# New orders of a step in a pipelined adapter, layer norm and conditional linear layer

## The chip, the cores and the metric

The kernel runs on one core of a Trainium2 chip. The metric is the time of one execution on the device in microseconds (us). Each core has TensorE (matmuls, PE), VectorE (DVE), ScalarE (ACT), GpSimd (POOL) and SyncE (SP), each with an instruction queue of its own that runs in order, and 16 DMA engines. The queues wait for one another through semaphores.

## What is computed

```python
# x is (32, 512, 512); two lists of 32 ids choose the weights of each sample
def reference(x, lang, cat, W1, b1, W2, b2, gamma, beta, W, b):
    h = relu(einsum('bsh,bha->bsa', x, W1[lang]) + b1[lang][:, None, :])      # a = 128
    y = x + einsum('bsa,bah->bsh', h, W2[lang]) + b2[lang][:, None, :]
    n = (y - mean(y)) * rsqrt(var(y) + 1e-5)
    x = x + n * gamma[lang][:, None, :] + beta[lang][:, None, :]
    return x + einsum('bti,bio->bto', x, W[cat]) + b[cat][:, None, :]          # W is 512 x 512
```

All is float32.

## The kernel before

A sample is 512 tokens by 512 features: four tiles of 128 tokens (NT = 4, index t) and four chunks of 128 features (NC = 4, index c). The kernel is a software pipeline over the 32 samples, written out by hand. Step k works on three samples at once: the adapter of sample k (up, relu, down, y, statistics), the norm and x1 of sample k - 1, and the linear layer of sample k - 2; besides it prepares sample k + 1. A step function stands in each engine's queue, and is called six times in a loop body (ROUND = 6), since buffers repeat after two or three samples: k.b is k mod 2, k.x is k mod 3. `k.count(per, back, more)` is the count that a semaphore has when "more" of the "per" events of sample k - back are done, so every wait names a sample. Steps 0 and 1 are written out separately ahead of the loops.

To get float32 out of fast matmuls, an operand is split in a high part (ScalarE, rounded to fp32r) and a low part (the rest, by GpSimd or VectorE), and a product is three matmuls: high x high, high x low, low x high (`split_product`, L837). This is done for x and w1 (three of four chunks, the fourth in plain float32, L882), h and w2, x1 and W.

**TensorE** (L927, not changed): linear tiles 0 and 1 of sample k - 2, up of sample k, the transposes of the norm of sample k - 1 for chunks 0 and 1 (`turn_norm`, L857), linear tile 2, down of sample k, transposes for chunks 2 and 3, linear tile 3. Tile 0 waits chunk by chunk for the low parts of x1 (L909), made by VectorE (L732) in the step before. PSUM has eight banks of which the linear layer uses o_bank 0 and 1 in turn, the norm n_bank 0 and 1 in turn.

**ScalarE** (L555): first part of W high (L511, two chunks at a time; it waits for GpSimd's `diag_done`), the norm of four tiles (L501), second part of W high, relu and h high (L528, L531), the issue of two of the four quarter loads of x for sample k + 2 (L591), x1 high for chunks 0 and 1 (L518), w2, w1 and x high for sample k + 1 (L486, L548, L553), squares of y for three tiles (L537), x1 high for chunks 2 and 3, the fourth square, the standard deviation (L542). In step 2 (`k.last(2)`) the norm comes first.

**VectorE** (L747): chunks 0 and 1 of the next x turned into the transposed layout xT (L667, from x_quad, which the quarter loads fill), output tile 0 (L744: bank plus b into out_half), chunks 2 and 3, output tile 1, x1 of chunk 0 (L726), h low (L672), x1 of chunk 1, x1 low for chunks 0 and 1 (L732), output tile 2, y and its means (L681, L687), x1 and x1 low for chunks 2 and 3, output tile 3, and last the statistics: `variance` and `inverse_deviation`, seven small instructions (L700 to L717) of which the second waits for all four squares and the third for the deviation.

**GpSimd** (L397): identity onto the diagonal of W (L405, which gives the residual), b2 onto x in two pairs of tiles (L423) with the low parts of W (L428) between and after, then w2, w1 and x low for sample k + 1 (L382, L388, L394).

**SyncE** (L281) issues the other loads and all stores: two quarters of x for sample k + 2, w1 and w2 of sample k + 1 (after the squares of sample k - 1), W of sample k, b2 and x of sample k + 1, b, the store of the first half of sample k - 2, then, after x1 of sample k - 1, the parameters gamma, beta and b1 of sample k + 1, and the store of the second half.

## Time and profile before

| | us |
|---|---|
| median of 3 runs (lowest, highest) | 615.1 (613.81, 616.61) |
| the profiled execution | 614.85 |
| its span, first to last instruction | 613.0 |

| engine | busy us | share of the span |
|---|---|---|
| TensorE matmuls | 606.5 | 99% |
| VectorE | 520.0 | 85% |
| GpSimd | 520.9 | 85% |
| ScalarE | 512.9 | 84% |
| DMA, mean of 16 engines | | 8 to 9 tenths in nearly all slices |

The clock granted to TensorE is 9 tenths or more in every slice (1.00 over nearly all of the span). 166.22 MB are moved, 271 GB/s on average. The page gives shares of the whole span; the stretches and single steps are read from the trace, where a line's rows tell its start, its length and, in brackets, the idle time of its engine before it and what ended that. A matmul's recorded end lies beyond the next one's start, as they are pipelined: only starts are compared.

### The profile page before, as it was taken

The page shows a single profiled execution, that of the slowest core. Times are in us where ns is not written, and L with a number is a line of the kernel's source. Part 1 is how long each engine was busy: PE and PEld are TensorE (multiplying, and loading weights), DVE is VectorE, ACT ScalarE, POOL GpSimd, SP SyncE. Part 2 cuts the span into 40 slices and gives each one's busy share as a digit, 9 for nine tenths or more (in the row PEclk, how much of TensorE's full clock was granted, in tenths as well). Part 3 has the DMA queues.
Part 4 walks back from the last instruction along what each step waited for, and adds up shares of the span by engine and source line. Part 5 has one row for each costly group of instructions (what it writes and reads, how often), then busy time and mean ns, then how long its engine had stood idle before and what let it go on. Part 6 is the DMA issues. An engine that isn't in the chain of part 4 may idle for free.

```text
span 613.0 us, 10710 instructions
## 1 busy us (share of the span) xinstructions
PE 606.5 (99%) x2863; PEld 488.4 (80%) x2863; DVE 520.0 (85%) x1151; ACT 512.9 (84%) x770; POOL 520.9 (85%) x263
## 2 busy tenths in 40 slices
PE   9999999999999999999999999999999999999998
PEld 7676787778888877787888888888888888888887
DVE  1799979889899889898888899899898889898673
ACT  4878888889888889889989889889888889889770
POOL 6778889899888899889999898899888899889830
PEclk9999999999999999999999999999999999999999
DMA  8989799887998898899898998888898898998422
GB/s 302 251 258 307 258 311 300 277 265 253 296 307 274 270 300 253 298 287 289 269 294 268 305 303 265 283 290 270 301 303 278 283 295 253 301 308 273 156 87 103
DMA packets 125938, 166.22 MB, mean 271 GB/s; under 512 B 11062, under 2 KB 72768, under 8 KB 121812
## 3 DMA queue, kind: packets, MB, share of 16 engines
q1 hardware_dynamic: 94900, 150.12, 75.2%
q10 hardware_dynamic: 30912, 15.73, 9.1%
q8 instruction: 10, 0.16, 0.1%
q14 instruction: 20, 0.16, 0.1%
q0 software_dynamic: 96, 0.05, 0.0%
HBM read 132.17 MB, written 33.55 MB: 270 GB/s over the span
## 4 chain that ended last, share of the span: by engine, by line
PE 75%; DMA 7%; ACT 6%; SPq 5%; DVE 3%; issue 3%; POOL 1%; ACTq 0%; DVEq 0%; POOLq 0%
PE o_bank L839 15%; PE o_bank L841 15%; PE o_bank L840 15%; PE n_bank L857 7%; DMA x_tok<-in_x 6%; PE d_bank L839 4%; PE d_bank L841 4%; PE d_bank L840 4%; PE d_bank L882 3%; ACT norm L501 2%; PE y_bank L839 2%; PE y_bank L841 2%; PE y_bank L840 2%; DVE x1T_lo L732 2%; DMA x_quad<-in_x 1%
## 5 line engine op out<-in xcount | busy, mean ns | idle before, releaser
L839 PE MATMUL o_bank<-w_hi,x1T_hi 128*128 128x512 f32 x512 | 205.6, 402 | 0.5 <-DVE x1T_lo L732 0.5
L841 PE MATMUL o_bank<-w_hi,x1T_lo 128*128 128x512 f32 x512 | 200.1, 391 | 0.0
L840 PE MATMUL o_bank<-w_lo,x1T_hi 128*128 128x512 f32 x512 | 199.1, 389 | 0.0
L428 POOL TENSOR_TENSOR w_lo<-w_raw,w_hi 128x1024 fp32r<-128x1024 f32 x62 | 149.1, 2404 | 10.0 <-ACT w_hi L511 9.8
L667 DVE STREAM_TRANSPOSE xT<-x_quad 128x512 f32<-128x512 f32 x120 | 127.2, 1101 | 34.1 <-DMA x_quad<-in_x 34.1
L501 ACT ACTIVATE norm<-y,neg_mean_rstd,rstd 128x512 f32<-128x512 f32 x128 | 152.2, 1266 | 1.1 <-DVE neg_mean_rstd L717 1.1
L423 POOL TENSOR_TENSOR x_tok<-x_tok,b_bc 128x1024 f32<-128x1024 f32 x60 | 145.0, 2416 | 5.4 <-DMA x_tok<-in_x 2.9
L518 ACT ACTIVATE x1T_hi<-n_bank,params 128x512 fp32r<-128x512 f32 x126 | 84.5, 688 | 34.7 <-DVE n_bank L726 29.5
L839 PEld LDWEIGHTS o_bank<-w_hi,x1T_hi 128*128 128x128 f32 x512 | 96.3, 188 | 21.1 <-issue 3.1
L841 PEld LDWEIGHTS o_bank<-w_hi,x1T_lo 128*128 128x128 f32 x512 | 96.1, 188 | 21.0
L840 PEld LDWEIGHTS o_bank<-w_lo,x1T_hi 128*128 128x128 f32 x512 | 96.4, 188 | 17.6
L537 ACT ACTIVATE x_tok<-y,neg_mean 128x512 f32<-128x512 f32 x128 | 91.8, 718 | 17.9 <-DVE neg_mean L687 17.8
L726 DVE SCALAR_TENSOR_TENSOR n_bank<-n_bank,params,xT 128x512 f32<-128x512 f32 x126 | 91.9, 754 | 10.1 <-PE n_bank L857 10.0
L394 POOL TENSOR_TENSOR xs_lo<-xT,xs_hi 128x1536 fp32r<-128x1536 f32 x28 | 98.7, 3525 | 0.0
L732 DVE SCALAR_TENSOR_TENSOR x1T_lo<-n_bank,params,x1T_hi 128x512 fp32r<-128x512 f32 x126 | 90.5, 748 | 9.3 <-ACT x1T_hi L518 4.5
L744 DVE TENSOR_TENSOR out_half<-o_bank,b_bc 128x512 f32<-128x512 f32 x127 | 85.4, 673 | 11.9 <-PE o_bank L841 11.7
L511 ACT ACTIVATE w_hi<-w_raw 128x1024 fp32r<-128x1024 f32 x64 | 67.7, 1061 | 18.2 <-POOL w_raw L405 17.4
L382 POOL TENSOR_TENSOR w_lo<-w_raw,w_hi 128x512 fp32r<-128x512 f32 x31 | 40.3, 1300 | 48.6 <-ACT w_hi L486 48.6
L857 PEld LDWEIGHTS n_bank<-ident,norm 128*128 128x128 f32 x504 | 58.9, 145 | 11.4 <-ACT norm L501 4.7
L857 PE MATMUL n_bank<-ident,norm 128*128 128x128 f32 x504 | 66.2, 274 | 0.6 <-ACT norm L501 0.5
L405 POOL TENSOR_TENSOR w_raw<-w_raw,ident 128x512 f32<-128x512 f32 x32 | 50.3, 1571 | 0.0
L681 DVE SCALAR_TENSOR_TENSOR y<-d_bank,x_tok 128x512 f32<-128x512 f32 x64 | 43.8, 684 | 1.1 <-PE d_bank L841 1.1
(95 smaller groups left out, 812.3 us busy)
## 6 DMA issues: line engine op xcount, KB each, us to landing
w_raw<-in_L_cond_W SPq DMA_DIRECT2D x32, 1024.0 KB, 6.6
out<-out_half SPq DMA_DIRECT2D x63, 512.0 KB, 4.5
x_tok<-in_x SPq DMA_DIRECT2D x31, 1024.0 KB, 11.4
w_raw<-in_L_cond_W SPq DMA_DIRECT2D x64, 256.0 KB, 4.3
b_bc<-in_L_cond_b SPq DMA_DIRECT2D x64, 256.0 KB, 8.7
x_quad<-in_x SPq DMA_DIRECT2D x62, 256.0 KB, 3.8
x_quad<-in_x ACTq DMA_DIRECT2D x58, 256.0 KB, 10.7
x_tok<-in_x ACTq DMA_DIRECT2D x2, 256.0 KB, 3.3
```

The source lines that it names most:

```text
L394: pool.tensor_tensor(xs_lo[:, :, :], xT[(k.x + 1) % 3][:, 0:NS, :], xs_hi[:, :, :].bitcast(F32), ALU.subtract).then_inc(xs_lo_done, 1)
L423: pool.tensor_tensor(pair, pair, b2_bc[p][:, :].rearrange("p (o h) -> p o h", o=1).to_broadcast([P, 2, H]), ALU.add).then_inc(x_b2_done, 2)
L428: pool.tensor_tensor(w_lo[q][:, c:c + 2, :], w_raw[q][:, c:c + 2, :], w_hi[q][:, c:c + 2, :].bitcast(F32), ALU.subtract).then_inc(w_lo_don ...
L501: act.activation(dst, src, ACT.Identity, scale=rstd[:, t:t + 1], bias=neg_mean_rstd[:, t:t + 1]).then_inc(norm_done, 1)
L537: act.activation(x_tok[k.b][:, t, :], y[:, t, :], ACT.Square, bias=neg_mean[:, t:t + 1], accum_out=sq_sum[:, t:t + 1]).then_inc(sq_done, 1)
L667: dve.transpose(xT[(k.x + 1) % 3][:, c, :].rearrange("p (b j) -> p b j", j=SQ), x_quad[1 - k.b][:, :, c::NC]).then_inc(xT_done, 1)
L726: dve.scalar_tensor_tensor(norm_bank(k, c)[:, :], norm_bank(k, c)[:, :], params[q][:, c:c + 1], xT[(k.x + 2) % 3][:, c, :], ALU.mult, ALU. ...
L732: dve.scalar_tensor_tensor(x1T_lo[q][:, c, :], norm_bank(k, c)[:, :], params[q][:, NC + c:NC + c + 1], x1T_hi[q][:, c, :].bitcast(F32), AL ...
L839: pe.matmul(acc, lhs_hi, rhs_hi, start=first, stop=False)
L840: pe.matmul(acc, lhs_hi, rhs_lo, start=False, stop=False)
L841: return pe.matmul(acc, lhs_lo, rhs_hi, start=False, stop=last)
L857: ins = pe.transpose(norm_bank(k, c)[:, t * P:(t + 1) * P], norm[:, t, c * P:(c + 1) * P] if by_chunk(k) else norm[:, t, c::NC], ident[:, :])
```

## The change

Five orders are changed; no matmul, no arithmetic and no byte of traffic is added or removed, but for a third small buffer of parameters.

- ScalarE: the norm whole, then w2's high part of the next sample, then both parts of W; the quarter loads leave its queue; all four squares and the deviation come ahead of x1's high parts of chunks 2 and 3.
- VectorE: output tile 0 and 1 each come ahead of a pair of turned chunks rather than behind it; h low behind x1 of chunk 1; the statistics ahead of x1's low parts of chunks 2 and 3.
- GpSimd: both sums of b2 and x first, then w2's low part, then both low parts of W, then w1's and x's as before.
- SyncE: w1 and w2 wait for down of sample k - 1; the wait for the squares stands ahead of b2 and x only; then the store of the second half of sample k - 3, b, the parameters (one of three buffers, waiting for x1 of sample k - 2), all four quarter loads of x, and the store of the first half of sample k - 2.
- Steps 0 and 1 keep their orders, but ScalarE issues no quarter loads there.

The core of the diff; the lines with @@ name the place.

```diff
@@ params: three buffers, and so three semaphores params_in
-        params = [sb(f"params{i}", [P, NP]) for i in range(2)]
+        params = [sb(f"params{i}", [P, NP]) for i in range(3)]
...
@@ SyncE, step
-                if quads:
-                    sp.wait_ge(xT_done, k.count(NC, 0, NC))
-                    load_x_quads(k.sample(-2), p)
                 if loads:
-                    sp.wait_ge(sq_done, k.count(NT, 0, 0))
+                    sp.wait_ge(down_done, k.count(NT, 0, 0))
                     load_w1(lang, q)
                     load_w2(lang, q)
                 if w_load:
...
                     load_w(cat_w, p)
                 if loads:
+                    sp.wait_ge(sq_done, k.count(NT, 0, 0))
                     load_b2(lang, q)
                     load_x(k.sample(-1), q)
+                if linear and k.since(3):
+                    store(k, 3, 1)
                 if turn:
...
                     load_b(cat_b, q)
+                if loads:
+                    if k.since(2):
+                        sp.wait_ge(x1_lo_done, k.count(NC, 1, 0))
+                    load_params(lang, (k.x + 1) % 3)
+                if quads:
+                    sp.wait_ge(xT_done, k.count(NC, 0, NC))
+                    load_x_quads(k.sample(-2), p)
                 if linear:
                     store(k, 2, 0)
-                if loads:
-                    sp.wait_ge(x1_lo_done, k.count(NC, 0, 0))
-                    load_params(lang, q)
-                if linear:
-                    store(k, 2, 1)
...
@@ GpSimd, step
                     if adapter:
                         plus_b2_pair(0)
+                        plus_b2_pair(2)
+                    if follow:
+                        low_w2(q, k.count(1, -1, 1))
                     if turn:
                         low_w_pair(0)
-                    if adapter:
-                        plus_b2_pair(2)
-                    if turn:
                         low_w_pair(2)
-                if follow:
-                    low_w2(q, k.count(1, -1, 1))
-                    if k.since(3):
+                    if follow and k.since(3):
                         low_w1(k)
                         low_xs(k)
...
@@ ScalarE, step
-                if k.last(2):
-                    for t in range(NT):
-                        normalise(k, t)
-                    high_w(k, 0)
-                else:
-                    high_w(k, 0)
-                    for t in range(NT):
-                        normalise(k, t)
+                for t in range(NT):
+                    normalise(k, t)
+                if follow:
+                    high_w2_of_next(k)
+                high_w(k, 0)
                 high_w(k, 2)
                 if adapter:
                     relu(k)
-                if follow and not k.last(S - 2):
-                    load_next_x_quads(k)
                 high_x1(k, 0)
                 high_x1(k, 1)
-                if follow:
-                    high_w2_of_next(k)
-                    if k.since(3):
-                        high_w1_of_next(k)
-                        high_xs_of_next(k)
+                if follow and k.since(3):
+                    high_w1_of_next(k)
+                    high_xs_of_next(k)
                 if adapter:
-                    square(k, 0)
-                    square(k, 1)
-                    square(k, 2)
+                    for t in range(NT):
+                        square(k, t)
+                    deviation(k)
                 high_x1(k, 2)
                 high_x1(k, 3)
-                if adapter:
-                    square(k, 3)
-                    deviation(k)
...
@@ VectorE, step
                 else:
+                    output(k, 0)
                     if follow:
                         turn_next_x(k, 0)
                         turn_next_x(k, 1)
-                    output(k, 0)
+                    output(k, 1)
                     if follow:
                         turn_next_x(k, 2)
                         turn_next_x(k, 3)
-                    output(k, 1)
                     x1(k, 0)
-                    if adapter:
-                        low_h(k)
                 x1(k, 1)
+                if adapter and not k.last(2):
+                    low_h(k)
                 low_x1(k, 0)
                 low_x1(k, 1)
                 output(k, 2)
...
                 x1(k, 2)
                 x1(k, 3)
+                if adapter:
+                    variance(k)
+                    inverse_deviation(k)
                 low_x1(k, 2)
                 low_x1(k, 3)
                 output(k, 3)
-                if adapter:
-                    variance(k)
-                    inverse_deviation(k)
```

## Rows read from the trace of the kernel before

**Rows 1.** Busy time in stretches: stretch, us, engines (instructions), clock, DMA share, GB/s

```profile
54.60:297.30 242.70, 242.12 (x1130) 192.96 (x1129) 214.78 (x470) 210.79 (x313) 218.70 (x105) 1.00 0.87 282
297.30:573.30 276.00, 276.00 (x1307) 224.86 (x1306) 245.50 (x540) 245.50 (x362) 252.00 (x121) 1.00 0.88 282
```

**Rows 2.** Timeline, TensorE: start us, us, what; feeding y, and R

```profile
433.12 0.39 PE L841 MATMUL d_bank<-w_hi,hT_lo 128*128 128x512 f32 x1
...
439.05 0.39 PE L839 MATMUL o_bank<-w_hi,x1T_hi 128*128 128x512 f32 x1
```

**Rows 3.** Waits (us, times, longest), 54 to 297 us, then 297 to 573 us

```profile
PEld n_bank L857 <- ACT norm L501: 4.0, 10, 0.9
...
DVE xT L667 <- DMA x_quad<-in_x: 16.6, 13, 1.9
```

**Rows 4.** Timeline, TensorE and VectorE: tile 0's first, x1T_lo, tile 1's first; two steps

```profile
198.24 0.39 PE L839 MATMUL o_bank<-w_hi,x1T_hi 128*128 128x512 f32 x1
...
198.46 1.41 DVE L732 SCALAR_TENSOR_TENSOR x1T_lo<-n_bank,params,x1T_hi 128x512 fp32r<-128x512 f32 x2
...
200.96 0.39 PE L839 MATMUL o_bank<-w_hi,x1T_hi 128*128 128x512 f32 x1
...
235.35 0.39 PE L839 MATMUL o_bank<-w_hi,x1T_hi 128*128 128x512 f32 x1
...
235.87 1.41 DVE L732 SCALAR_TENSOR_TENSOR x1T_lo<-n_bank,params,x1T_hi 128x512 fp32r<-128x512 f32 x2
...
238.24 0.39 PE L839 MATMUL o_bank<-w_hi,x1T_hi 128*128 128x512 f32 x1
```

**Rows 5.** Timeline, VectorE, the step of R = 420.65: x1, low_h, y, low_x1

```profile
429.75 0.76 DVE L726 SCALAR_TENSOR_TENSOR n_bank<-n_bank,params,xT 128x512 f32<-128x512 f32 x1 [0.47 <-PE n_bank L857]
...
430.55 0.69 DVE L672 TENSOR_TENSOR hT_lo<-d_bank,hT_hi 128x512 fp32r<-128x512 f32 x1
...
433.98 0.68 DVE L681 SCALAR_TENSOR_TENSOR y<-d_bank,x_tok 128x512 f32<-128x512 f32 x1
...
438.40 1.41 DVE L732 SCALAR_TENSOR_TENSOR x1T_lo<-n_bank,params,x1T_hi 128x512 fp32r<-128x512 f32 x2
```

**Rows 6.** Timeline, ScalarE's squares in that step; sample 0's last square and statistics

```profile
435.44 0.72 ACT L537 ACTIVATE x_tok<-y,neg_mean 128x512 f32<-128x512 f32 x1 [0.49 <-DVE neg_mean L687]
...
436.16 0.71 ACT L537 ACTIVATE x_tok<-y,neg_mean 128x512 f32<-128x512 f32 x1
...
18.46 0.72 ACT L537 ACTIVATE x_tok<-y,neg_mean 128x512 f32<-128x512 f32 x1
...
20.45 0.16 DVE L717 TENSOR_TENSOR neg_mean_rstd<-d_bank,rstd 128x4 f32<-128x4 f32 x1
```

**Rows 7.** Timeline of step 2: ScalarE's W parts, VectorE, and TensorE's wait

```profile
37.85 2.00 ACT L511 ACTIVATE w_hi<-w_raw 128x1024 fp32r<-128x1024 f32 x2
...
41.05 0.69 DVE L672 TENSOR_TENSOR hT_lo<-d_bank,hT_hi 128x512 fp32r<-128x512 f32 x1 [0.73 <-ACT hT_hi L531]
...
45.14 0.68 DVE L681 SCALAR_TENSOR_TENSOR y<-d_bank,x_tok 128x512 f32<-128x512 f32 x1
...
49.48 1.41 DVE L732 SCALAR_TENSOR_TENSOR x1T_lo<-n_bank,params,x1T_hi 128x512 fp32r<-128x512 f32 x2
...
50.38 0.47 PE L839 MATMUL o_bank<-w_hi,x1T_hi 128*128 128x512 f32 x1 [0.49 <-DVE x1T_lo L732]
```

**Rows 8.** Start: VectorE's first turn of sample 2; DMA traffic from 19 to 36 us

```profile
22.46 1.10 DVE L667 STREAM_TRANSPOSE xT<-x_quad 128x512 f32<-128x512 f32 x1 [1.85 <-DMA x_quad<-in_x]
...
DMA packets 4171, 4.50 MB, mean 265 GB/s; under 512 B 471, under 2 KB 3015, under 8 KB 4039
```

**Rows 9.** The page's groups and DMA issues, whole span

```profile
L501 ACT ACTIVATE norm<-y,neg_mean_rstd,rstd 128x512 f32<-128x512 f32 x128 | 152.2, 1266 | 1.1 <-DVE neg_mean_rstd L717 1.1
...
L428 POOL TENSOR_TENSOR w_lo<-w_raw,w_hi 128x1024 fp32r<-128x1024 f32 x62 | 149.1, 2404 | 10.0 <-ACT w_hi L511 9.8
...
x_quad<-in_x ACTq DMA_DIRECT2D x58, 256.0 KB, 10.7
```

More of the change, by code:

```diff
@@ L338, in _ @@
                          ).then_inc(first_b1_in[1], 16)
-            load_x_quads(2, 0, range(NQ))
+            load_x_quads(2, 0)
             sp.wait_ge(table_done, 1)
@@ L357, in _ @@
             last = Step(S // ROUND, 3)
+            store(last, 3, 1)
             store(last, 2, 0)
```

33 lines of the change are left out of this document (14 added, 19 removed).

## The prediction

> **What bounds the kernel now.** I read, in this order, the busy time in four stretches, the waits of the same stretches, one step on each engine in the timeline, then the first 55 us.
>
> From 297.3 to 573.3 us TensorE is busy for 276.0 of 276.0 us over 15 steps (1307 matmuls, 87 in a step): 18.40 us a step, no gap. From 54.6 to 297.3 us 13 steps take 242.7 us, 18.67 each [rows 1]. So the later half stands at TensorE's own work, and the change, which takes no matmul away, can win only what the earlier half has over it: 242.7 - 13 x 18.40 = 3.5 us. I count offsets in a step from R, the first matmul of tile 0 of the linear layer: R is 439.05 in one step and 420.65 in the one before [rows 2]. The earlier half loses its 3.5 us in two places: the weight loads of the norm's transposes waited 4.0 us for ScalarE's norm, ten times, and tile 0's third chunk waited for VectorE's x1T_lo [rows 3, 4]. In the later half VectorE waits 16.6 us for x_quad [rows 3], about 1.1 us a step, but TensorE has no gap there, so this wait costs nothing.
>
> The second place has a limit that can be read. With the third x1T_lo started at R + 0.22 (198.46) tile 0 takes its usual 2.72 us. Started at R + 0.52 (235.87) it takes 2.89, 0.17 more [rows 4]. So TensorE loses s - 0.35 us when that instruction starts s behind R. In the step at 439.05 it starts at 438.40, s = -0.65: a full microsecond of room [rows 2, 5].
>
> **The parts of the change.**
>
> Norm ahead of W's first part (ScalarE), statistics ahead of x1's last parts (VectorE), W's parts last on GpSimd. The norm no longer waits for the high part of W, which waits for GpSimd's diagonal, and its scale comes some 2 us earlier. The waits on the norm go. Worth at most the 3.5 us; part of that is the other place, and one of the 13 steps lost nothing, so I take 3.0.
>
> GpSimd keeps every instruction. The new wait is that of w2's low part for w2's high part, now ahead of both parts of W; behind it stand W's low parts and w1's and x's. Norm ends near offset 5.5, w2's high part at 6.0, then GpSimd needs 1.2 us for w2 (half as wide as a part of W) and 2 x 2.4 for W [rows 9], and is at w1 near 12.0, which is when it comes. Cost nothing: W's low part is needed only in the next step (18.4). If that cover goes it costs what GpSimd is late, from 6 us on.
>
> ScalarE: the two quarter loads leave it (whose issue held x1's high part back), and the fourth square and the deviation move ahead of x1's third and fourth high part. Nothing there becomes late: x1's high parts then end near 19.0, the norm's four instructions (1.27 us on average, [rows 9]) end at 24.0, that is 5.6 of the next step, and the first x1 behind their transposes stands at 9.10.
>
> VectorE: the first output now precedes the first two turns. It waits for tile 0 (near 2.9) and then two turns, an output and two turns end near 8.2, before x1 can start at 9.10 (429.75) [rows 2, 5]. Nothing.
>
> Then the one part that lies on the path: the five small instructions of the statistics, with their waits for all four squares, now stand **ahead of the third x1T_lo**, whose room is 1.0 us. Worked out from x1 at 9.10: two in a row take 1.41 us of 0.75 each, so a successor starts 0.09 before the recorded end [rows 5]. x1 twice 1.32, low_h 0.60, low_x1 twice 1.32, output 0.60: y starts at 12.94. The matmul that feeds it starts at 12.47 and is 0.39 long [rows 2], so it is ready. Before, y started at 13.33 (433.98), as x1's high parts were late. The first square starts 1.46 behind y (435.44 - 433.98), the second 0.72 behind it [rows 5, 6]; the third waits for the second pair's mean, 2.97 behind y; the fourth at 16.63. The statistics' last product starts 1.99 us after the fourth square where nothing else stands between (18.46 to 20.45 in the first sample), and the next instruction starts 0.09 before its end, 0.08 behind its start, as it is 0.16 long [rows 6]. The third x1T_lo then starts at 16.63 + 2.07 = 18.70, that is s = 0.30, against the limit of 0.35. **The room of 1.0 us is used up but for 0.05.** Both numbers are good to about 0.1. From below the cost is 0; from above, with s = 0.55, 0.2 us in each of 28 steps, 5.6 us. It can't gain, as TensorE has no gap to give. I take 0.02 a step, 0.5 us, since a few steps will lie beyond. It is a loop: y waits for TensorE, which waits for x1T_lo, so a loss is paid in every step.
>
> The first steps. In step 2 the room doesn't exist: TensorE already waits 0.49 us there for x1T_lo, started at 49.48, 4.34 us behind y (45.14) [rows 7]. In the new order it is 3.69 + 2.07 = 5.76 behind y: **1.4 us later**, and nothing hides it. Besides, low_h in this step waited for ScalarE (0.73 us, at 41.05) [rows 7], and in ScalarE's queue w2's high part for sample 3 now stands ahead of both parts of W and of the relu. In before it came after. Its own slot is 0.5 us (an estimate: a square of the same size starts 0.72 behind the last with its accumulator's read in between, [rows 6]); it also waits for w2 to land. SyncE now issues w1, w2, W, b2, x, b, then sample 3's four quarters, then step 2's w1 and w2: 4.5 MB behind sample 2's quarters, which were in at 22.46. At 265 GB/s that is 17 us: 39.4, where ScalarE is there at 37.85 [rows 7, 8]. A wait of 1 to 1.5 us, of which I take 1.2. Bounds: 0 if w2 overtakes the quarters, 2.5 if the queue is no faster than 230 GB/s. So step 2 costs 1.4 + 0.5 + 1.2 = **3.1 us**, bounds 1.9 and 4.4, and TensorE never makes it good.
>
> All quarters on SyncE, behind x, b and the parameters. ScalarE's took 10.7 us to land [rows 9], being issued last of 4 MB. Now they are issued near offset 4 of a step and wanted at 3.5 of the next, 18 us later, so VectorE's wait for them goes, worth nothing. SyncE's queue: the four issues stand ahead of the store of half 0 and of the next step's w1 and w2, which aren't wanted until 15 us later. The second half's store waits for the last output at about 2.2 and holds b and the parameters back, both of which have a step of room. The third parameter buffer takes a wait away and costs nothing. The Trainium skill (DMA: Bandwidth & Descriptors, "Issuing engines are not separate DMA queues" and "Queues, rings and completion order") says that transfers of both engines run on the same 16 DMA engines and that within one ring they are taken in order. By that rule no bandwidth is won, and what is issued behind the quarters waits for them; it speaks for the late w2 in step 2, and against the bound of 0 there (by the rule alone the sum would keep its 1.2 us).
>
> End: after the last step TensorE runs without a wait; the new order of stores changes nothing of the last one.
>
> **Sum.** The profiled execution took 614.85 us, its span 613.0, against a median of 615.1. 614.85 - 3.0 + 3.1 + 0.5 = 615.4 us. So the change wins in the earlier half what it pays in step 2.
>
> **The rivals.**
>
> Statistics decide (slower): s is not 0.30 but 0.45 to 0.65, from waits on semaphores that my spacings leave out. It decides from s = 0.35 on. At s = 0.50 it is 28 x 0.15 = 4.2 us, 619.1 us. For it: the room is 0.05 us. Against it: every spacing is a measured one.
>
> The start is cheap: w2 lands in time or the order in step 2 costs half. 614.85 - 3.0 + 1.0 to 1.9 = 612.9 to 613.8 us. For it: the landing is estimated from a mean rate, and transfers differ much in theirs.
>
> Full gain: the stall in step 2 is absent, as work shifts beside it, and the 3.5 us come back: 611.4 us. Against it: y to x1T_lo in that step is a plain chain.
>
> One queue for all loads: the quarters block SyncE's queue, stores land late, and the output that reuses the half waits. A half is stored again 9 to 10 us after its issue at offset 2.3; ahead of it lie 2.75 MB of loads, about 10 us at 265 GB/s. It decides once the queue is 2 us later than I take it; 0.2 us a step would give 28 x 0.2 = 5.6 us, 621.0 us.
>
> That the orders do nothing (the earlier half keeps its loss from transfers, step 2 pays): 618.4 us.
>
> **How the numbers follow.** A measurement of this kernel tells about 0.5%, 3.1 us, from no change. Forecast 0.47, statistics 0.20, cheap start 0.15, full gain 0.08, queue 0.04, orders do nothing 0.06. All of the forecast and most of the cheap start lie within 3.1 us of 615.1; the full gain and a few in a hundred of the cheap start are faster; statistics, queue and half of the last are slower. That gives 0.12 faster, 0.62 same, 0.26 slower. The range 612.2 to 619.8 reaches over the cheap start and over most of the statistics case, and leaves out the full gain and the queue.
>
> **What would show it.** Steps from 75 us on of 18.40 us, with no wait on the norm. The third x1T_lo at s near 0.3; beyond 0.35 each step is longer by the excess. In step 2 TensorE's wait for x1T_lo near 2 us, low_h near 42.8 rather than 41.05, w2's high part waiting for a DMA, and the first up behind it near 57.6 rather than 54.6. VectorE's wait for x_quad gone. The prediction is wrong if a new wait of GpSimd on w2 reaches TensorE, if s misses by more than 0.1, or if w2 lands before 37.9.

## The result and the profile after the change

The changed kernel takes **618.14 us** (median of 5 runs, 615.9 to 618.49), the kernel before 613.81 us beside it: ratio 1.006, 95% interval 1.0031 to 1.0089. It is slower, by a little over the 0.5% that can be told, and 2.7 us above the forecast of 615.4. Against the kernel before the miss is larger: the forecast added 0.6 us to the profiled execution's 614.85, and 4.3 us were added to the 613.81 measured beside it. The profiled execution took 618.28 us, its span 616.5.

| first "up" matmul of a step, us | step 2 | step 3 | step 4 | last | 27 steps from step 4 on | span |
|---|---|---|---|---|---|---|
| before | 28.96 | 54.58 | 73.49 | 573.30 | 499.81 | 613.0 |
| after | 31.33 | 58.78 | 77.68 | 576.76 | 499.08 | 616.5 |
| difference | +2.4 | +4.2 | +4.2 | +3.5 | -0.7 | +3.4 |

So the whole loss, and more, is there 78 us into the run: 2.4 us in the start, 1.8 in step 2. The other 27 steps give 0.7 back, where 2.5 was forecast. Busy time in stretches (stretch, us, engines with their instructions, granted clock, DMA share, GB/s), of the kernel after, which answer to [rows 1] but for the first:

```profile
20.00:30.00 10.00, 8.03 (x39) 6.43 (x38) 6.29 (x17) 7.49 (x12) 6.08 (x6) 0.83 0.96 265
54.60:297.30 242.70, 242.69 (x1140) 196.15 (x1141) 219.15 (x474) 211.48 (x315) 218.89 (x105) 1.00 1.03 286
297.30:573.30 276.00, 274.37 (x1297) 222.42 (x1296) 247.13 (x539) 238.78 (x360) 249.32 (x120) 1.00 1.00 279
```

The first of these in the kernel before:

```profile
20.00:30.00 10.00, 8.56 (x53) 7.17 (x52) 7.86 (x22) 8.49 (x14) 6.04 (x6) 1.00 0.96 253
```

The earlier half, the one the change aimed at, now holds 1140 matmuls in place of 1130 and has no gap. The later half, full before, holds ten fewer (1297 for 1307) and has a gap of 1.6 us. In the start the granted clock is 0.83, where it was 1.00. The start and step 2 on TensorE (start us, us, what, and in brackets the idle time ahead of it and what ended it):

```profile
24.99 0.50 PE L824 MATMUL d_bank<-w_hi,hT_hi 128*128 128x512 f32 x1 [1.98 <-DVE hT_lo L657]
...
28.35 0.63 PE L825 MATMUL d_bank<-w_lo,hT_hi 128*128 128x512 f32 x1
28.77 0.63 PE L826 MATMUL d_bank<-w_hi,hT_lo 128*128 128x512 f32 x1
...
44.68 0.50 PE L824 MATMUL d_bank<-w_hi,hT_hi 128*128 128x512 f32 x1 [0.56 <-DVE hT_lo L657]
...
54.58 0.47 PE L824 MATMUL o_bank<-w_hi,x1T_hi 128*128 128x512 f32 x1 [1.79 <-DVE x1T_lo L717]
```

TensorE was idle for 1.98 us ahead of the down projection of step 1 (1.44 before), ran at full speed for 1.7 us, and then at the lower of its two levels: matmuls 0.42 us apart (28.35 to 28.77) instead of 0.23, from 26.6 to 29.2 us (1.2 in place of 2.4 GHz). Then VectorE and ScalarE in the same stretch, which answer to [rows 7] and [rows 8]:

```profile
23.27 1.10 DVE L652 STREAM_TRANSPOSE xT<-x_quad 128x512 f32<-128x512 f32 x1 [2.37 <-DMA x_quad<-in_x]
...
40.20 0.63 ACT L493 ACTIVATE w_hi<-w_raw 128x512 fp32r<-128x512 f32 x1
...
43.94 0.69 DVE L657 TENSOR_TENSOR hT_lo<-d_bank,hT_hi 128x512 fp32r<-128x512 f32 x1 [1.52 <-ACT hT_hi L538]
...
48.03 0.68 DVE L666 SCALAR_TENSOR_TENSOR y<-d_bank,x_tok 128x512 f32<-128x512 f32 x1
...
53.70 1.40 DVE L717 SCALAR_TENSOR_TENSOR x1T_lo<-n_bank,params,x1T_hi 128x512 fp32r<-128x512 f32 x2
```

The third x1T_lo of step 2 starts 5.67 us behind y (forecast 5.76, before 4.34). Its wait is the 1.79 us of TensorE. The high part of w2 (40.20) hardly waits: w2 landed at 40.18, and ScalarE was free at 40.07, 2.2 us later than before.

A step of the later half, tile 0's first matmul (R) at 442.56, which answers to [rows 2, 5, 6]:

```profile
433.25 1.42 DVE L711 SCALAR_TENSOR_TENSOR n_bank<-n_bank,params,xT 128x512 f32<-128x512 f32 x2 [0.70 <-PE n_bank L842]
...
437.08 0.69 DVE L666 SCALAR_TENSOR_TENSOR y<-d_bank,x_tok 128x512 f32<-128x512 f32 x1
...
440.86 0.71 ACT L544 ACTIVATE x_tok<-y,neg_mean 128x512 f32<-128x512 f32 x1
...
442.56 0.39 PE L824 MATMUL o_bank<-w_hi,x1T_hi 128*128 128x512 f32 x1
...
442.91 1.40 DVE L717 SCALAR_TENSOR_TENSOR x1T_lo<-n_bank,params,x1T_hi 128x512 fp32r<-128x512 f32 x2
```

The chain came out as forecast: y 3.83 us behind x1 (forecast 3.84), the fourth square 3.78 behind y (forecast 3.69), the third x1T_lo 2.05 behind that (forecast 2.07). It starts at s = 442.91 - 442.56 = 0.35, 0.27 in the steps outside the loop (forecast 0.30). Such steps last 18.41 and 18.37 us. The waits from 77 to 577 us (us in total, times, longest), which answer to [rows 3]:

```profile
POOL w_lo L389 <- ACT w_hi L493: 44.3, 27, 3.1
...
DVE out_half L729 <- DMA out<-out_half: 2.1, 2, 1.4
PE o_bank L824 <- DVE x1T_lo L717: 1.6, 2, 1.2
```

VectorE's wait for x_quad and TensorE's for the norm are gone. GpSimd's wait for w2's high part, which the prediction calls new, was there before at nearly the same size: 48.6 us over the whole span, against 52.9 now. From the page of the kernel before:

```profile
L382 POOL TENSOR_TENSOR w_lo<-w_raw,w_hi 128x512 fp32r<-128x512 f32 x31 | 40.3, 1300 | 48.6 <-ACT w_hi L486 48.6
```

New is that VectorE's output waited twice for a store. TensorE's gap in the later half follows from that, and SyncE's queue shows why (issues of DMAs; start, length, what):

```profile
351.68 0.41 SPq L282 DMA_DIRECT2D out<-out_half  x1
...
353.55 8.63 SPq L247 DMA_DIRECT2D x_quad<-in_x  x4
...
428.93 4.36 SPq L247 DMA_DIRECT2D x_quad<-in_x  x4
433.38 2.24 SPq L282 DMA_DIRECT2D out<-out_half  x1
```

```profile
363.00 0.69 DVE L729 TENSOR_TENSOR out_half<-o_bank,b_bc 128x512 f32<-128x512 f32 x1 [1.44 <-DMA out<-out_half]
```

The store of the second half, issued at 351.68 behind w1, w2, W, b2 and x in the same queue, landed at 362.90, after 11.2 us (the median of the stores on the page is 8.1, and was 4.5 before), and the output that writes this half again, the third of the step, waited 1.44 us for it. How full the queue is can be seen in the issues themselves: the four quarters take SyncE 4.36 us in the step shown, 5.4 in the median step, and 8.63 in this one. In the kernel before SyncE's two quarters cost 0.90 us (and ScalarE's two 0.95):

```profile
425.41 0.90 SPq L243 DMA_DIRECT2D x_quad<-in_x  x2
```

The page's rows that answer to [rows 9] (line, engine, operation, count | busy us, mean ns | idle before; and the DMA's issues with KB and us to landing):

```profile
L508 ACT ACTIVATE norm<-y,neg_mean_rstd,rstd 128x512 f32<-128x512 f32 x128 | 152.3, 1265 | 1.1 <-DVE neg_mean_rstd L702 1.1
...
L435 POOL TENSOR_TENSOR w_lo<-w_raw,w_hi 128x1024 fp32r<-128x1024 f32 x62 | 147.5, 2402 | 12.1 <-ACT w_hi L518 12.1
...
x_quad<-in_x SPq DMA_DIRECT2D x120, 256.0 KB, 9.1
```

No large group of instructions has become longer by more than 2% on average.

### The profile page after: what moved, and what is told of

It is laid out like the page before. It is cut to its first block, busy times and chain, and to the rows that moved or that the text cites. A ratio compares the mean times of both kernels' runs of the same rounds, so it can differ in the third digit from the quotient of the medians.

```text
span 616.5 us, 10723 instructions
## 1 busy us (share of the span) xinstructions
PE 606.5 (98%) x2863; PEld 490.2 (80%) x2863; DVE 525.1 (85%) x1151; ACT 506.4 (82%) x770; POOL 520.8 (84%) x263
## 4 chain that ended last, share of the span: by engine, by line
PE 86%; DMA 5%; DVE 4%; ACT 2%; issue 2%; SPq 1%; DVEq 0%; ACTq 0%
PE o_bank L824 17%; PE o_bank L826 17%; PE o_bank L825 17%; PE n_bank L842 8%; PE d_bank L824 5%; PE d_bank L826 5%; PE d_bank L825 5%; PE d_bank L867 4%; DMA out<-out_half 4%; PE y_bank L824 2%; PE y_bank L826 2%; PE y_bank L825 2%; PE d_bank L855 1%; ACT x_tok L544 1%; DMA w_raw<-in_L_cond_W 1%
## 5 line engine op out<-in xcount | busy, mean ns | idle before, releaser
L435 POOL TENSOR_TENSOR w_lo<-w_raw,w_hi 128x1024 fp32r<-128x1024 f32 x62 | 147.5, 2402 | 12.1 <-ACT w_hi L518 12.1
L729 DVE TENSOR_TENSOR out_half<-o_bank,b_bc 128x512 f32<-128x512 f32 x127 | 86.8, 684 | 33.1 <-PE o_bank L826 30.7
L711 DVE SCALAR_TENSOR_TENSOR n_bank<-n_bank,params,xT 128x512 f32<-128x512 f32 x126 | 89.0, 753 | 20.9 <-PE n_bank L842 20.9
L717 DVE SCALAR_TENSOR_TENSOR x1T_lo<-n_bank,params,x1T_hi 128x512 fp32r<-128x512 f32 x126 | 88.3, 743 | 0.6 <-ACT x1T_hi L525 0.5
L525 ACT ACTIVATE x1T_hi<-n_bank,params 128x512 fp32r<-128x512 f32 x126 | 80.0, 682 | 9.0 <-DVE n_bank L711 7.6
L389 POOL TENSOR_TENSOR w_lo<-w_raw,w_hi 128x512 fp32r<-128x512 f32 x31 | 40.5, 1306 | 52.9 <-ACT w_hi L493 52.9
L518 ACT ACTIVATE w_hi<-w_raw 128x1024 fp32r<-128x1024 f32 x64 | 64.1, 1056 | 0.0
```

Source lines behind the costliest of these rows:

```text
L435: pool.tensor_tensor(w_lo[q][:, c:c + 2, :], w_raw[q][:, c:c + 2, :], w_hi[q][:, c:c + 2, :].bitcast(F32), ALU.subtract).then_inc(w_lo_don ...
L711: dve.scalar_tensor_tensor(norm_bank(k, c)[:, :], norm_bank(k, c)[:, :], params[(k.x + 2) % 3][:, c:c + 1], xT[(k.x + 2) % 3][:, c, :], AL ...
L717: dve.scalar_tensor_tensor(x1T_lo[q][:, c, :], norm_bank(k, c)[:, :], params[(k.x + 2) % 3][:, NC + c:NC + c + 1], x1T_hi[q][:, c, :].bitc ...
```

## The experiments

The theory after the result: the loss has two places, the start and step 2, and the gain in the later steps is small because most executions of the kernel before don't have the loss that the profiled one had. The rival: the steps pay, by the statistics ahead of x1T_lo or by the one queue. Each experiment is compared with runs of the kernel before on its own chip: 613.28 us (17 runs) for the first four, 613.03 (23) for the next four, 613.72 (35) for the last four.

**The changed kernel again.** No edit.

> The changed kernel once more, beside the kernels that it is compared with. Account so far, from its first trace, against the kernel before (span 616.5 against 613.0, +3.4): start up to step 2's first up matmul +2.4 (of which 1.5 under a granted clock of half), step 2 +1.8, the 27 steps after it -0.7 (the 3.0 of the earlier half and 0.8 of a slightly shorter step won, 0.5 lost to statistics in time, 2.6 lost in four steps where VectorE waited for a store). If the start is chance, the span varies with the clock: 614 to 615 us at clock 1.00. If it belongs to the change, the clock is under 1.00 in nearly every run and the first up of step 2 stands near 31.3 us again. Ratio 1.004 to 1.008.

Measured: 618.25 us, ratio 1.0079 (1.0055 to 1.0104). In its trace:

```profile
26.47 0.79 PE L824 MATMUL d_bank<-w_hi,hT_hi 128*128 128x512 f32 x1 [3.66 <-DVE hT_lo L657]
...
56.90 0.47 PE L824 MATMUL o_bank<-w_hi,x1T_hi 128*128 128x512 f32 x1 [1.81 <-DVE x1T_lo L717]
```

```profile
79.97:576.98 497.01, 496.99 (x2350) 403.68 (x2349) 445.25 (x971) 433.51 (x649) 452.99 (x216) 1.00 1.02 283
```

The start is worse here (3.66 us idle, clock 0.78 from 20 to 30 us, step 3 at 61.07). Step 2 takes 27.13 us, 1.5 more than in the kernel before, with the same wait for x1T_lo (1.81 us). The 27 steps take 497.01 us without a wait for a store, and the clock was under 1.0 in 5 of these 6 runs, as expected if the start belongs to the change. The store waits come in some executions alone: of the ten traces here that keep the change's order of stores, the first has 2.1 us of them, one more 0.24 us, the others none. Of the four long steps that the expectation puts down to them, two (18.64 and 18.49 us) hold no such wait and are long in this trace too.

**Step 2 in the old order.** VectorE, ScalarE and GpSimd keep the old place of statistics, fourth square and w2's parts in this one step.

```
-                if adapter:
+                if adapter and not k.last(2):
                     variance(k)
                     inverse_deviation(k)
                 low_x1(k, 2)
                 low_x1(k, 3)
                 output(k, 3)
+                if k.last(2):
+                    variance(k)
+                    inverse_deviation(k)
```

> The changed kernel with step 2 alone in the old order (statistics behind x1's low parts, w2's high and low part late, fourth square late), all other steps new. My theory (step 2 is a fill cost of its own, of statistics ahead of x1's low parts and of w2 in ScalarE's queue): step 2 shrinks from 27.45 to about 25.6 us, the whole by 1.8 to 2.5 us against the changed kernel. The rival (step 2 is late only because the start was late, and its length is set by transfers): no change, 0.5 us at most.

Measured: 615.26 us, ratio 1.0028 (1.001 to 1.0046), 3.0 us less than the changed kernel on that chip.

```profile
49.58 0.68 DVE L674 SCALAR_TENSOR_TENSOR y<-d_bank,x_tok 128x512 f32<-128x512 f32 x1
...
53.92 1.41 DVE L725 SCALAR_TENSOR_TENSOR x1T_lo<-n_bank,params,x1T_hi 128x512 fp32r<-128x512 f32 x2
```

```profile
54.81 0.47 PE L835 MATMUL o_bank<-w_hi,x1T_hi 128*128 128x512 f32 x1 [0.52 <-DVE x1T_lo L725]
...
74.64 0.47 PE L835 MATMUL o_bank<-w_hi,x1T_hi 128*128 128x512 f32 x1 [0.31 <-DVE x1T_lo L725]
```

y to x1T_lo is 4.34 us again, as in the kernel before, and step 2 takes 25.37 us for the 27.13 of the repeat. But step 3 takes 19.84 for 18.90: its norm, now whole and first, waits 1.40 us for statistics that come late, and TensorE waits once more for x1T_lo. In the trace the edit saves 1.76 - 0.94 = 0.8 us; the medians give 3.0. What the medians have beyond it goes with the clock: it was 1.0 or 0.999 in 6 of these 12 runs (five at 1.0 with a median of 613.76) and in 1 of the 6 of the changed kernel. Step 2's order can't act on the clock of the stretch ahead of it, so part of the 3.0 is likely chance among few runs.

**Statistics last in all steps.** VectorE's statistics and ScalarE's fourth square and deviation go behind x1's last parts again; the norm stays whole and first.

```
                 x1(k, 2)
                 x1(k, 3)
-                if adapter:
-                    variance(k)
-                    inverse_deviation(k)
                 low_x1(k, 2)
                 low_x1(k, 3)
                 output(k, 3)
+                if adapter:
+                    variance(k)
+                    inverse_deviation(k)
```

> The changed kernel with the statistics back behind x1's low parts and the last output on VectorE, and the fourth square and deviation back behind x1's high parts on ScalarE, in all steps; norm still ahead of W. My theory (the statistics use up a room of 1.0 us, so that every small delay on VectorE reaches TensorE): the third x1T_lo starts about 0.65 us ahead of tile 0 instead of 0.27 behind it, no step is over 18.45 us, the store waits of VectorE remain but cost nothing; step 2 is 1.4 us shorter. Together 3.5 to 4.5 us less than the changed kernel. The rival (norm is late without the early statistics, or the excess steps come from the queue alone): steps of 18.5 to 18.7 remain, and at most 1.5 us is won.

Measured: 621.81 us, ratio 1.0136 (1.0113 to 1.0158), 3.6 us more than the changed kernel where 3.5 to 4.5 less was expected. The theory that this order costs in the steps fell: s does drop to -0.37, but steps take 18.5 to 18.6 us. Waits from 60 to 577 us:

```profile
ACT norm L508 <- DVE neg_mean_rstd L705: 39.5, 28, 1.5
...
DVE hT_lo L660 <- ACT hT_hi L538: 23.2, 27, 1.1
...
PEld d_bank L827 <- DVE hT_lo L660: 8.6, 24, 0.6
```

ScalarE stands at the norm, and all behind it in its order (w2, both parts of W, the relu) is late, until TensorE waits for hT_lo. So the two orders belong together: with the norm whole and first, the early statistics are needed.

**Two quarter loads back on ScalarE**, behind its relu; the loads of a step on SyncE stay where the change put them. In step 1 ScalarE issues its two behind w2's high part.

```
+                if follow and not k.last(S - 2):
+                    load_next_x_quads(k)
                 high_x1(k, 0)
...
             high_w2_of_next(k1)
+            load_next_x_quads(k1)
```

> The changed kernel with two of the four quarter loads back in ScalarE's queue behind the relu, as before; all else new. Two theories give opposite signs. If the limit of the third x1T_lo is real (a step longer by its start less 0.35 us), the issue holds x1's high part back by 0.4 us, x1T_lo starts near 0.65, and each of 28 steps is 0.3 us longer: 6 to 9 us more than the changed kernel, with no wait for a store. If instead the one queue is what costs, this undoes it and wins 2 to 3 us.

Measured: 628.18 us, ratio 1.0248 (1.0225 to 1.0271), 9.9 us more than the changed kernel. Timeline and stretches:

```profile
51.05 0.79 PE L838 MATMUL d_bank<-w_hi,hT_hi 128*128 128x512 f32 x1 [8.35 <-DVE hT_lo L671]
```

```profile
48.35 2.08 DVE L666 STREAM_TRANSPOSE xT<-x_quad 128x512 f32<-128x512 f32 x2 [9.44 <-DMA x_quad<-in_x]
```

```profile
40.00:50.00 10.00, 2.70 (x12) 1.88 (x10) 1.65 (x2) 2.22 (x4) 10.00 (x6) 0.88 1.13 270
297.30:573.30 276.00, 275.90 (x1297) 221.65 (x1296) 246.67 (x538) 240.21 (x360) 250.99 (x120) 1.00 1.00 283
```

ScalarE's two quarters of sample 3, issued in step 1 at 33.63 and 34.00, landed at 43.76 and 48.33, VectorE stood 9.44 us for them, and step 2 took 35.48 us. That is 8.4 us over the repeat's 27.13, and most of what was lost. The number came near the 6 to 9 us expected, but from a cause that the expectation doesn't have: the 27 steps, to which it gave the loss, took 500.88 us, 3.9 over the repeat, and the start was 4.3 shorter (first up of step 2 at 29.68 for 33.94). There was no wait for a store. The DMA engines' share stayed at 0.99 to 1.00 in the later steps and a store's median landing at 8.3 us, though the quarters are on two queues again.

The later steps settle the limit of [rows 4] on more points: in this and the other traces s = 0.27, 0.35, 0.45, 0.65, 0.86 goes with steps of 18.37, 18.41, 18.47, 18.67, 18.85 us. The excess over 18.37 is 0.04, 0.10, 0.30, 0.48, that is s - 0.35, to 0.03. It is a lower bound where other waits come on top, as in many steps of the run with the store first, below.

**The low part of h first in the start.**

```
-            turn_next_x(k1, 0)
             low_h(k1)
+            turn_next_x(k1, 0)
             turn_next_x(k1, 1)
```

> The changed kernel with one line of the start moved: VectorE makes sample 1's low part of h before it turns sample 2's first chunk, so that down no longer waits for sample 2's last quarter load. My theory (in the changed kernel that quarter lands at 23.2 to 24.7 us instead of 22.4, TensorE stands idle 2.0 to 3.7 us instead of 1.4, and the clock granted to it falls to half behind the longer idle time, 1.5 to 3 us more): TensorE waits under 1 us there, the clock is 1.00 in all runs, step 2's first up matmul stands near 28 us instead of 31.3 to 33.9, and the whole is 2.5 to 4 us less than the changed kernel, 614.5 to 615.5 us. The rival (the clock falls for another cause, and the start is caught up later): clock under 1.00 in most runs again, at most 1 us won.

Measured: 617.85 us, ratio 1.007 (1.0042 to 1.0097): 0.4 below the changed kernel's repeat, far less than expected. The start has no idle of note in this trace and its first up of step 2 stands at 28.09, as expected, but:

```profile
45.41 0.50 PE L824 MATMUL d_bank<-w_hi,hT_hi 128*128 128x512 f32 x1 [3.45 <-DVE hT_lo L657]
```

```profile
40.93 0.63 ACT L493 ACTIVATE w_hi<-w_raw 128x512 fp32r<-128x512 f32 x1 [3.03 <-DMA w_raw<-in_L_cond_W]
```

Here is the wait for w2 that the prediction put into step 2, and larger: ScalarE is there at 37.90, w2 lands at 40.9. In the changed kernel it was hidden by the late start. The two don't add up; take one away and the other comes forward. The clock was 1.0 in 1 of the 6 runs and 0.994 to 0.997 in the others, so both signs of the expectation's rival (clock under 1.00 in most runs, at most 1 us won) came true. That the start's idle time is what lowers the clock is therefore not shown by this run alone; the wait of 3.45 us may do it in the other executions, and in the run below that takes both under 1 us the clock is 1.0 in 10 of 12.

**The second half's store first.**

```
+                if linear and k.since(3):
+                    store(k, 3, 1)
                 if loads:
                     sp.wait_ge(sq_done, k.count(NT, 0, 0))
                     load_b2(lang, q)
                     load_x(k.sample(-1), q)
-                if linear and k.since(3):
-                    store(k, 3, 1)
```

> The changed kernel with SyncE's store of the second half of sample k - 3 ahead of the loads of b2 and x instead of behind them. My theory (VectorE's output waits for this store behind 2.75 MB of loads in one queue, 0.6 to 1.4 us in a few steps, and as the room is gone each wait reaches TensorE): no wait of VectorE for a store, no step over 18.5 us but one or two, 0.5 to 2.5 us less than the changed kernel. The rival (it is the amount of traffic, not its order, that makes these steps long): the long steps remain, or x arrives late on GpSimd, no gain.

Measured: 637.29 to 653.6 us in six runs, with a median of 645.18; the ratio, 1.0424 (1.038 to 1.0468), is taken from the three shortest of them (median 640.12). It is the opposite of what I expected. Waits from 60 to 577 us of an execution of 650.5 us:

```profile
DVE out_half L729 <- DMA out<-out_half: 59.8, 25, 5.6
...
ACT w_hi L493 <- DMA w_raw<-in_L_cond_W: 25.0, 19, 3.8
```

The store waits for an output, SyncE with it, and b2, x, b, parameters and quarters go out later in every step. The next step's store and w2 are then late. So stores and loads that hold one another up on SyncE are a mechanism that works; how near the changed kernel is to it is not shown.

**Sample 3's quarters first in step 1**, ahead of w1 on SyncE, in this step alone.

```
+                if k.last(1):
+                    sp.wait_ge(xT_done, k.count(NC, 0, NC))
+                    load_x_quads(k.sample(-2), p)
                 if loads:
                     sp.wait_ge(down_done, k.count(NT, 0, 0))
                     load_w1(lang, q)
...
-                if quads:
+                if quads and not k.last(1):
```

> The changed kernel with sample 3's four quarter loads ahead of w1, w2 and W in SyncE's step 1 alone, as the kernel before had two of them; all other steps new. It tells why sample 2's last quarter lands late. My theory (the loads issued next behind it decide it: quarters behind quarters leave it at 22.4 us, w1, w2 and W take bandwidth from it): it lands near 22.5 us, TensorE's idle time is 1.4 to 1.6 us and the clock 1.00, the start is 1.5 to 2.5 us shorter; but W and x come 3 us later, which step 2 may pay. The rival (it lands late by chance of that run or by the new code): 23 to 24.7 us again and clock under 1.00.

Measured: 615.57 us, ratio 1.0038 (1.0018 to 1.0057), 2.3 us less than the 617.85 of the run beside it, the clock at 1.0 in 7 of 12 runs.

```profile
24.82 0.50 PE L827 MATMUL d_bank<-w_hi,hT_hi 128*128 128x512 f32 x1 [1.57 <-DVE hT_lo L660]
...
30.54 1.98 PE L858 MATMUL d_bank<-xT,w_raw 128*128 128x512 f32 x4 [0.78 <-DMA w_raw<-in_L_cond_W]
```

1.57 us idle, and the clock stays at 1.00 from 20 to 30 us. But the quarter landed at 23.07, not near 22.5, so the theory that the loads behind it decide its landing fell. And w1 now stands behind four quarters, and TensorE waits 0.78 us for it.

**The kernel before with the low part of h first.** The same edit of the start as above, in the kernel before.

> The kernel before with the same line of the start moved (low part of h ahead of the turn), nothing of the change. It has an idle time of 1.4 us there at full clock. If that idle time is plain loss: 1 to 1.5 us less than the kernel before, near 612 us, clock 1.00. If step 2 is bound by ScalarE's and VectorE's own chains anyway: no difference.

Measured: 613.17 us, ratio 0.9991 (0.9973 to 1.0008), no difference. The first up of step 2 comes 0.9 us earlier (28.04 for 28.96), and by step 3 that is gone (54.48 for 54.58). What the run shows is the loop. 27 steps of the kernel before, in the execution of the prediction and in this one:

```profile
73.49:573.30 499.81, 499.23 (x2351) 403.40 (x2350) 442.22 (x972) 440.06 (x650) 453.55 (x217) 1.00 0.88 282
```

```profile
73.70:570.87 497.17, 497.11 (x2351) 404.49 (x2350) 442.41 (x971) 440.64 (x650) 453.81 (x217) 1.00 0.88 284
```

The same code in the loop takes 499.81 us in one execution and 497.17 in another, in which most steps take 18.40. The changed kernel's 497.01 is hardly less.

**Step 2 old, and sample 3's quarters first.** Both edits above.

> The changed kernel with two edits together: sample 3's quarter loads first on SyncE in step 1 alone, and step 2 alone in the kernel before's order of statistics and w2's high part. Theory (the loss has two places, the start with its half clock and step 2, and the earlier half of every later step is worth next to nothing): the loss of the two places goes together, the first up matmul of step 3 starts at 55.5 to 56.5 us (57.72 with the first edit alone), the time is 612.5 to 613.8 and the granted clock 1.0 in most runs. Rival (the edits remove the same wait twice, as their single results of -3.0 and -2.7 each already reach 615.3 to 615.6): 615 to 616. Second rival (the orders inside the steps are worth 3 us once start and step 2 are mended, as the prediction had it): 610 to 611.

Measured: 614.95 us, ratio 1.002 (1.0002 to 1.0037). The time misses what was expected by over a microsecond and stands beside the first rival's 615 to 616. Step 3 starts at 55.05, earlier than expected, but takes 19.73 us for 18.90, as in the run with step 2 alone. Clock 1.0 in 6 runs (median 613.7), 0.997 in 6 (615.8).

**Step 2 old, and the low part of h first.**

> The changed kernel with the start's low part of h ahead of the turning of sample 2, and step 2 alone in the kernel before's order. Theory (w2's high part pinned ahead of W's in ScalarE is what held step 2 in the run with the first edit alone, by the 3.03 us that it waited for w2 to land): TensorE's 3.45 us idle ahead of down of step 2 goes, the first up of step 3 starts at 56 to 57 us, the time is 612.5 to 614 with the granted clock 1.0 in most runs. Rival (the late landing of sample 3's quarters, which both edits leave behind b on SyncE, decides step 2): idle of 2 to 3 us stays at another place, and the time is 615 to 616.5, no better than with step 2 alone.

Measured: 614.92 us, ratio 1.0031 (1.0008 to 1.0054), 0.9 above what was expected, with the clock at 1.0 in 10 of 12 runs. TensorE's idle ahead of down falls from 3.45 to 0.97 us, as the theory has it (ScalarE no longer stands at w2), and step 3 starts at 56.26. Yet step 3 takes 20.09:

```profile
72.16 0.47 PE L835 MATMUL o_bank<-w_hi,x1T_hi 128*128 128x512 f32 x1 [0.64 <-DVE x1T_lo L725]
```

With the clock full, 1.2 us of loss against the kernel before is left, and it lies in steps 2 and 3: the clock is not the whole of it.

**All three edits.** The loop stays as the change has it.

> All three edits together: start's low part of h first, sample 3's quarters first on SyncE in step 1, step 2 alone in the kernel before's order; the later steps stay wholly as the change has them. Theory: first up of step 3 at 54.6 to 55.5 us, time 611.5 to 613, within 0.5% of the kernel before, because the 27 periods from step 4 on take the same 497 to 499 us in both kernels. Rival (earlier half of each step worth 3 us): 609.5 to 610.5, faster by 0.4 to 0.6%.

Measured: 613.27 us, ratio 0.9983 (0.9965 to 1.0), not to be told from the kernel before, and 0.3 above what was expected. Clock 1.0 in 7 of 12 runs. Step 3 starts at 56.37, 0.9 later than expected. The trace still holds a loss ahead of step 4 (75.57 against 73.49):

```profile
30.11 3.61 PE L869 MATMUL d_bank<-xT,w_raw 128*128 128x512 f32 x4 [2.05 <-DMA w_raw<-in_L_cond_W]
```

The quarters ahead of w1 delay w1 by 2.05 us now that TensorE comes for it in time, and behind this wait the granted clock was 0.83 from 30 to 40 us. The 27 steps take 497.18 us. So the changed kernel's loss of 0.6 to 0.8% lies in the start and step 2 (an edit of step 2 moves part of it to step 3), and with most of it mended the new orders of the later steps win about what is left of it.

**SyncE's step 1 alone, in the kernel before.** Its two quarter loads of sample 3 go behind the load of b.

```
-                if quads:
+                if quads and not k.last(1):
                     sp.wait_ge(xT_done, k.count(NC, 0, NC))
                     load_x_quads(k.sample(-2), p)
...
                     load_b(cat_b, q)
+                if k.last(1):
+                    sp.wait_ge(xT_done, k.count(NC, 0, NC))
+                    load_x_quads(k.sample(-2), p)
```

> The kernel before with one thing changed, in step 1 alone: SyncE's two quarter loads of sample 3 go from the head of the step to behind the load of b; all else stays. Theory (the order of SyncE in step 1 sets when sample 2's last quarter lands, by what is put on the queue ahead of or beside it, and with it TensorE's idle time and clock in the start): the last quarter of sample 2 lands at 23.0 to 24.7 us instead of 22.44, TensorE is idle 2 us or more ahead of down of step 1, the granted clock of the 20 to 30 us window is under 0.9, and the time is 1.5 to 3 us above the kernel before: 614.5 to 616. Rival (it is the changed kernel's one queue for all quarters that lands them late, not their order in step 1): no difference that can be measured, 612.5 to 613.7.

Measured: 613.43 us, ratio 1.0007 (0.9982 to 1.0032). My theory of the start fell:

```profile
24.58 0.53 PE L842 MATMUL d_bank<-w_hi,hT_hi 128*128 128x512 f32 x1 [1.21 <-DVE hT_lo L675]
```

Sample 2's last quarter lands at 22.81, TensorE is idle for 1.21 us, the clock stays at 1.00. The order of SyncE in step 1 by itself doesn't spoil the start. What does is **open**. That quarter landed at 22.44, 22.81 and 23.16 in three traces with the kernel before's program, and at 22.87 to 24.72 in the eleven traces of the changed kernel and its variants (median 23.2), though it is issued at 13.6 to 14.4 in all fourteen. The expectation's rival, the one queue for all quarters, can't be it: the kernel before too has all four quarters of sample 2 on SyncE, behind the same loads, and ScalarE's first quarter load goes out only at 32.91.

What the traces do show is that these same loads kept the DMA engines busier, in the kernel before (first row) and after:

```profile
18.00:22.00 4.00, 4.00 (x21) 2.60 (x20) 1.41 (x10) 2.99 (x8) 3.72 (x3) 1.00 0.95 197
...
18.00:22.00 4.00, 4.00 (x20) 2.52 (x19) 1.69 (x10) 3.00 (x7) 4.00 (x4) 1.00 1.18 189
```

Here nearly all that moves is these quarters. The share is 0.95 to 0.99 in the three traces with the kernel before's program and 1.13 to 1.23 in the eleven others. In the traces' packet records, from 100 to 560 us, the quarters' packets (512 bytes) take 31 ns on average in those three and 44 to 52 in these eleven, while packets of 2048 bytes take 98 to 104 in all. What all eleven have from the start on, and the three don't, is the third parameter buffer. It is declared right ahead of x_quad, and may shift x_quad and all that follows in memory. That this is the cause is a rival that no run tests; the kernel before with an unused third buffer would test it.

The 27 steps took 499.75 us here, so two of the three traces of the old loop have that loss; but this execution took 615.16 us, 1.7 above its own median. Seven of the eight traces with the change's later steps left as they are took 497.0 to 497.4 us.

## Why the prediction was right and wrong

**What bounds the kernel**: right. Steps stand at TensorE's own work in both kernels.

**Norm first, W last, worth 3.0 us**: the waits on the norm went, as forecast. The size was right against the execution it was read from (499.81 - 497.01 = 2.8, where the forecast, less its 0.5 for the statistics, was 2.5) and wrong as a gain on the median. That execution took 614.85 us, 1.0 to 1.8 above the medians of 613.0 to 613.8 that the kernel before showed later, and one of three executions of its loop had next to nothing of the loss. An estimate for the median one: 613.7 us on the last occasion, less 1.8 outside the span, 39.7 behind the last up and 73.7 ahead of step 4 leave 498.5 for the 27 steps, so the gain is 1.4 us. This is the first mis-sized term. In the changed kernel's own profile 2.1 us went to store waits besides.

**GpSimd, ScalarE and the first output cost nothing**: right. But GpSimd's wait for w2's high part isn't new, as the prediction has it: it was 48.6 us before and is 52.9 now, and nobody waited for it. That the third parameter buffer "costs nothing" was given without a reason and isn't shown (the rival above).

**Statistics ahead of x1T_lo**: right to 0.1 us, s = 0.27 to 0.35 against 0.30, and so was the limit of 0.35. The cost came out at 1.0 us at most for the 0.5 forecast (497.01 less 27 steps of 18.37): 0.02 to 0.05 in an ordinary step of the loop, and 0.1 to 0.3 in three steps, six apart, which the forecast lacked. Against that, a step without a wait takes 18.37 us where it took 18.40, 0.8 us in 27 steps, which the forecast lacked too. The "statistics decide" rival (619.1 us) is out: the time is near, the mechanism isn't there.

**The first steps, 3.1 us**: the first term, 1.4 us for the statistics, came as forecast (y to x1T_lo 5.67 for 5.76; TensorE waited 1.79 us, for 0.49 + 1.4 = 1.89). The slot of w2's high part (0.5 us) fits the 0.56 us that TensorE waited for hT_lo at 44.68, and was absent in the repeat. The wait for w2 to land (1.2 us) didn't show, because ScalarE came 2.2 us late. The run with the start mended showed it at 3.03 us: w2 lands at 40.9, where I had put 39.4. Step 2 measured +1.8 us, and +1.5 in the repeat.

**What the prediction lacked is the start itself.** It put no cost ahead of step 2. There, the last quarter of sample 2 came 0.8 to 2.3 us later, in front of an hT_lo that TensorE was already waiting for, and behind the idle time the clock fell: +2.4 us in one trace, +5.0 in the other. [rows 8] held the wait of 1.85 us for that quarter; I used the row for a mean rate, not for what hangs on it. For the clock's part, the runs of the kernel before beside these give a price: 62 of 75 had it at 1.0, with medians of 613.3, 612.9 and 613.6 us on the three occasions, and 9 at 0.997, with medians of 615.7 and 616.0. Of the changed kernel's 11 runs 2 had 1.0. Why the quarter came late stays open. So it is in part luck that 618.1 lies within 612.2 to 619.8: the range was drawn for a cheap start and for late statistics, and what moved the time was a stretch without a term in the sum. The rival that the orders do nothing (618.4 us, chance 0.06) met the number as well, but not by its mechanism: step 2 paid 1.8 us and not 3.1, and the earlier half kept nothing of its loss.

**All quarters on SyncE**: the bandwidth was no help, as forecast, and the wait for x_quad went, worth nothing. The rule that the prediction took from the Trainium skill (DMA: Bandwidth & Descriptors, "Issuing engines are not separate DMA queues") adds that issuing from several engines only saves the sequencer's time, "usually small relative to the DMA itself". This case differs: four quarter issues held SyncE for 4.1 to 8.6 us of an 18.4 us step, where two took 0.90 us, and 1.2 us with the other two back on ScalarE and the order otherwise as changed. The store waits of the "one queue" rival, with a chance of 0.04, did come about, in two of ten traces and with 2.1 and 0.24 us rather than 5.6; that the number of queues is behind them is not shown, since stores landed no sooner with two queues (8.3 us for 8.1).

**The sum**, in the profiled executions: start +2.4 (forecast 0), step 2 +1.8 (3.1), later steps -0.7 (-2.5), together +3.4 (+0.6).

## What to carry to other kernels

A gain that is read from one execution's stretch is worth no more than that execution has over the median; look at a second one, or subtract. Ahead of the steady steps, follow each load to the instruction that it frees and to what stands behind that in the same queue, since an idle time of TensorE there can be paid twice, the second time in its clock. Two waits in one place hide each other: sum them as a chain, and expect the second when the first is mended.

## What the runs showed of the hardware

TensorE's clock in the start, by the idle time ahead of down of step 1: 1.21, 1.28, 1.44, 1.48 and 1.57 us idle went with 1.00 from 20 to 30 us, 1.98, 2.07 and 2.18 with 0.83, 3.43 with 0.76, 3.66 with 0.78. It isn't the idle time alone: 3.45 us ahead of down of step 2 (the low part of h first) left the clock at 1.00 in that trace, while 2.05 us ahead of step 2 (all three edits) gave 0.83 from 30 to 40 us, and the 8.35 us with the quarters on ScalarE gave 0.88 and then 0.78.

The same bytes took a larger share of the DMA engines' time in the changed kernel: 1.00 to 1.04 in the later steps against 0.87 to 0.88 before, at 279 to 286 GB/s against 282 to 284. The number of queues doesn't explain it, since the share stayed at 0.99 to 1.00 with two quarters back on ScalarE. The time lies in the quarters' packets of 512 bytes (44 to 52 ns for 31), and their cause is open.

The issues of the four quarters took SyncE from 0.35 to 3.4 us each, and all that stands behind them on that engine moved with them.
